# Two rings of three PSUM banks, and one common list of parts, in the slice-weight stage of a graph-network kernel

## The chip, the cores and the metric

The kernel is one program on one core of a Trainium2 chip, launched once. The metric is device time in microseconds (us) from start to end; lower is better. The core has a tensor engine (PE, with its weight loads shown apart as PEld), a vector engine (DVE), a scalar engine (ACT), GpSimd (POOL) and the queue of the sync engine (SP) that issues most of the transfers. Each engine works through its own list of instructions in order and waits for the others on semaphores.

## The reference, cut to what matters

The whole program is two blocks of a graph network on 6250 nodes of 256 features: graph attention, linear attention, a mixture of experts, a relational layer, and at the end a "slice attention". Only the first part of the last one is touched:

```python
# x: [6250, 256], layer-normalised; H = 8 heads, G = D = 64
fx_mid = (x @ W_fx + b_fx)                      # [N, 512]
x_mid  = (x @ W_x + b_x)                        # [N, 512]
slice_weights = softmax((x_mid @ W_slice + b_slice) / temp, axis=-1)
slice_norm  = slice_weights.sum(axis=2)
slice_token = einsum('bhnc,bhng->bhgc', fx_mid, slice_weights)
# then attention among the 64 tokens of each head, and
out_x = einsum('bhgc,bhng->bhnc', out_slice, slice_weights) @ W_out + b_out
```

The kernel has folded W_x, W_slice and the temperature into one matrix of 256x512 beforehand, so a tile of nodes needs one product for its logits, a softmax over groups of 64, and a sum of (features x weights) over all nodes.

## The kernel before

The nodes stand in 50 tiles of 128 rows, two tiles make a pair, and five pairs (slots u = 0 to 4) make a round; there are five rounds. All work of the stage is in `slice_weights`. For each pair and round r there are these parts, and each part runs over the five slots:

- norm: DVE takes the statistics of the loaded rows (L493, L500), ACT the square root (L505), DVE the reciprocal (L509) and the scaled rows xn (L514).
- turn: PE transposes xn into a PSUM bank (L538), ACT copies it to xt (L3542).
- logit0 and logit1, for the first and the second tile of the pair: PE multiplies xt with the logit matrix into a bank (L3594, two matmuls of 128x512); DVE adds the bias out of the bank (L3496), takes the maximum (L3499), subtracts it (L3502); ACT takes the exponential (L3546); DVE sums it (L3505), inverts the sum (L3508) and scales (L3512).
- sum0 and sum1, for the two tiles: PE adds features times weights into the two accumulating banks sum_bank (L3602, two matmuls), and then transposes the weights into a bank (L3610, four transposes); ACT copies that out to slice_t (L3550), which the last stage reads.
- copy: ACT copies xn to xs (L3554), which sum0 and sum1 read.

Of the eight PSUM banks, two are sum_bank, five are `bank[u]`, one for each slot, shared in turn by turn, logit0 and logit1, and one is `turn_bank`, through which all transposes of sum0 and sum1 go one at a time.

The order of the parts on each engine is written out by hand. In the loop, with r the finished round and r+1 the one begun, PE has logit1(r), sum0(r), turn(r+1), logit0(r+1), sum1(r); DVE has norm(r+1), logit1(r), logit0(r+1); ACT has the root of norm(r+1), the copies of sum0(r), turn(r+1), the exponentials of logit1(r), three copies of sum1(r), the exponentials of logit0(r+1), the other two copies of sum1(r), and copy(r+1). The file has two helpers that other stages use and this one does not: `rounds`, which lays out a list of parts on an engine, and `Ring`, which deals a few banks to the slots of several parts in turn.

Of the kernel before, what the change touches and what calls it, by code (L numbers as in the profile page):

```python
# [14 lines left out]
P = 128  # L15
# [3389 lines left out]
def slice_weights(nc, io, dram, keep, logit, tokens, slice_t, sums):  # L3405
# [5 lines left out]
    ALL, HEAD, REST = range(U), range(3), range(3, U)  # L3411
    with ExitStack() as stack:
# [13 lines left out]
        bank = [space.ps(f"bank{u}", [P, 512]) for u in range(U)]  # L3426
        turn_bank = space.ps("turn_bank", [P, 512])
# [6 lines left out]
            space.sems(n, PAIR) for n in ("s_lg", "s_lb", "s_mx", "s_sub", "s_exp", "s_sm", "s_rc", "s_sw", "s_swt", "s_swtc"))  # L3434
        tiles = pair_rows(dram["x3"])
# [16 lines left out]
        with nc.Block() as block:  # L3452
# [17 lines left out]
            def _(dve):  # L3470
# [9 lines left out]
                def part(name, r):  # L3480
# [11 lines left out]
                    elif name in ("logit0", "logit1"):  # L3492
                        i = int(name[-1])
                        for u, n in slots(r):
                            dve.wait_ge(s_lg[i], n)
                            nc.vector.tensor_tensor(sw[:, u, i], bank[u][:, :], b_logit[:, :], ALU.add).then_inc(s_lb[i], 1)  # L3496
# [17 lines left out]

                part("norm", (0, 0))
                part("logit0", (0, 0))
                with dve.Fori(0, ROUNDS - 1) as r:
                    part("norm", (r, 1))
                    part("logit1", (r, 0))
                    part("logit0", (r, 1))  # L3520
                part("logit1", (ROUNDS - 1, 0))
# [8 lines left out]
            def _(act):  # L3530
# [5 lines left out]
                def part(name, r, chosen=ALL):  # L3536
                    for u, n in [slots(r)[k] for k in chosen]:
                        if name == "norm":
                            ln.root(nc, u, n)
                        elif name == "turn":  # L3540
                            act.wait_ge(s_xt, n)
                            nc.scalar.copy(xt[:, u].rearrange("p a n -> p (a n)"), bank[u][:, :]).then_inc(s_xtc, 1)  # L3542
                        elif name in ("logit0", "logit1"):
                            i = int(name[-1])
                            act.wait_ge(s_sub[i], n)
                            nc.scalar.activation(sw[:, u, i], sw[:, u, i], ACT.Exp).then_inc(s_exp[i], 1)  # L3546
                        elif name in ("sum0", "sum1"):
                            i = int(name[-1])
                            act.wait_ge(s_swt[i], n + U)
                            nc.scalar.copy(slice_t[:, tile_at(r, u, i), :].rearrange("p t n -> p (t n)"), turn_bank[:, :]).then_inc(s_swtc[i], 1)  # L3550
                        elif name == "copy":
                            act.wait_ge(s_xn, n + U)
                            act.wait_ge(s_swt[1], n)
                            nc.scalar.copy(xs[:, u, :, 0:D - 1], xn[:, u, :, 0:D - 1]).then_inc(s_copied, 1)  # L3554

                for name in ("norm", "turn", "copy", "logit0"):
                    part(name, (0, 0))
                with act.Fori(0, ROUNDS - 1) as r:
                    part("norm", (r, 1))
                    part("sum0", (r, 0))  # L3560
                    part("turn", (r, 1))
                    part("logit1", (r, 0))
                    part("sum1", (r, 0), HEAD)
                    part("logit0", (r, 1))
                    part("sum1", (r, 0), REST)
                    part("copy", (r, 1))
                part("sum0", (ROUNDS - 1, 0), HEAD)
                part("logit1", (ROUNDS - 1, 0))
                part("sum0", (ROUNDS - 1, 0), REST)
                part("sum1", (ROUNDS - 1, 0))  # L3570

            @block.tensor
            def _(pe):
# [6 lines left out]
                def part(name, r):  # L3580
                    for u, n in slots(r):
                        if name == "turn":
                            pe.wait_ge(s_lb[1], n)
                            pe.wait_ge(s_xn, n + U)
                            transpose_pair(nc, bank[u], xn[:, u], keep["ident"]).then_inc(s_xt, 1)
                        elif name in ("logit0", "logit1"):
                            i = int(name[-1])
                            b = bank[u]
                            if i == 0:
                                pe.wait_ge(s_xtc, n + U)  # L3590
                            else:
                                pe.wait_ge(s_lb[0], n + U)
# [4 lines left out]
                        elif name in ("sum0", "sum1"):  # L3597
# [5 lines left out]
                            if u:  # L3603
                                pe.wait_ge(s_swtc[i], n - 1 + U)
                            elif i == 0:
                                pe.wait_ge(s_swtc[1], n - 1 + U)
                            else:
                                pe.wait_ge(s_swtc[0], n - 1 + U + U)
                            for j in range(J):
                                last = nc.tensor.transpose(turn_bank[:, j * P:(j + 1) * P], sw[:, u, i, j * P:(j + 1) * P], keep["ident"][:, :])  # L3610
                            last.then_inc(s_swt[i], 1)

                part("turn", (0, 0))
                part("logit0", (0, 0))
                with pe.Fori(0, ROUNDS - 1) as r:
                    part("logit1", (r, 0))
                    part("sum0", (r, 0))
                    part("turn", (r, 1))
                    part("logit0", (r, 1))
                    part("sum1", (r, 0))  # L3620
                for name in ("logit1", "sum0", "sum1"):
                    part(name, (ROUNDS - 1, 0))
# [300 lines left out]
```

## Time and profile before

| | us |
|---|---|
| median of 3 runs | 7020.97 (7016.3 to 7034.65) |
| the profiled execution | 7016.3 |
| its span | 7014.5 |
| the loop of the stage and its last round on DVE (6680.36 to 6866.40) | 186.04 |
| mean granted clock of TensorE | 0.864 of full |

Over the whole span PE is busy 75%, DVE 69%, ACT 59% and POOL 52%. These shares average many stages; the stage changed here lies near the end, from about 6642 to 6880 us. After it come only the small work on the tokens and the output. In the rows below the granted clock (PEclk) is 1.00 at 2.4 GHz and 0.50 at 1.2 GHz, the two levels it has.

### The profile page before, as it was taken

The numbers are of one execution on the slowest core, as the hardware profiler recorded it, in microseconds if no ns is written. First come the engines' busy times: TensorE is split into PE (matmuls) and PEld (weight loads), VectorE is DVE, ScalarE is ACT, GpSimd is POOL, SyncE is SP. The second block draws the span as 40 slices with busy tenths as digits, with TensorE's granted clock in tenths as the row PEclk, the third lists the DMA queues.
The fourth block names the chain that finished last, engine by engine and source line by source line (L and its number), as shares of the span: only waits on it lengthen the run. The fifth ranks groups of instructions, "written<-read, shape, count | busy, mean of one in ns | idle before, by whom it ended". The sixth has DMA issues, their size and how long they took to land. (4 is left out here: it accounts for less than half of the span.)

```text
span 7014.5 us, 94498 instructions
## 1 busy us (share of the span) xinstructions
PE 5285.4 (75%) x22314; PEld 3780.4 (54%) x22314; DVE 4842.0 (69%) x13222; ACT 4141.8 (59%) x13411; POOL 3626.7 (52%) x3571
## 2 busy tenths in 40 slices
PE   1768888655888887558888624999998787778698
PEld 1645555434555564535555313888884466555446
DVE  5756666695777777767777687666662487777693
ACT  4568888874899898668998873333335322111142
POOL 3377777727777774477777710000000477777501
PEclk8878888876899998678999866999999898888799
DMA  6444444444444443454444432000006644333402
GB/s 178 120 129 117 118 118 116 111 126 143 117 123 119 123 121 99 129 149 119 125 119 121 112 105 79 28 18 18 18 18 221 206 117 125 109 110 103 128 23 75
DMA packets 483983, 763.48 MB, mean 109 GB/s; under 512 B 85543, under 2 KB 360695, under 8 KB 483511
## 3 DMA queue, kind: packets, MB, share of 16 engines
q0 software_dynamic: 166320, 446.82, 23.3%
q1 hardware_dynamic: 317335, 313.36, 14.2%
q14 instruction: 253, 2.07, 0.1%
q8 instruction: 75, 1.23, 0.1%
HBM read 622.82 MB, written 146.27 MB: 110 GB/s over the span
## 5 line engine op out<-in xcount | busy, mean ns | idle before, releaser
L1806 POOL DMA_INDIRECT gm_got<-scratch_feat,keep_src_tab x2490 | 2485.7, 998 | 776.2 <-issue 668.9
L2028 ACT ACTIVATE gm_got<-gm_got 128x64 f32<-128x64 f32 x9828 | 2393.7, 335 | 5.5 <-DVE gm_got L1941 5.5
L2083 PE MATMUL gm_bank<-gm_got,gm_onehot 128*128 128x264 f32 x4980 | 1777.0, 464 | 401.9 <-DVE gat_acc L1966 236.0
L2083 PEld LDWEIGHTS gm_bank<-gm_got,gm_onehot 128*128 128x128 f32 x4980 | 934.3, 216 | 911.8 <-DVE gat_acc L1966 360.3
L1966 DVE TENSOR_TENSOR gat_acc<-gat_acc,gm_bank 128x264 f32 x2490 | 1060.1, 426 | 506.4 <-PE gm_bank L2083 240.2
L1114 POOL DMA_INDIRECT mix1a_got<-scratch_rel_feat,layer_rel_tab x240 | 238.1, 992 | 1524.8 <-issue 1524.5
L1114 POOL DMA_INDIRECT mix1b_got<-scratch_rel_feat,layer_rel_tab x590 | 583.8, 989 | 189.9 <-issue 186.0
L1171 PE MATMUL mix1b_m_bank<-mix1b_got,mix1b_onehot 128*128 128x256 f32 x1180 | 380.0, 456 | 154.3 <-DVE layer_acc L1145 129.8
L837 POOL DMA_INDIRECT scratch_first<-gat_scores,keep_first_pos x150 | 224.7, 1498 | 461.5 <-DVE gat_scores L820 420.1
L1973 DVE TENSOR_TENSOR gm_onehot<-keep_iota_row,keep_dst_tab 128x896 f32<-128x896 f32 x357 | 386.8, 1084 | 25.8 <-PE gm_bank L2083 22.2
L1171 PEld LDWEIGHTS mix1b_m_bank<-mix1b_got,mix1b_onehot 128*128 128x128 f32 x1180 | 241.0, 222 | 261.1 <-DVE mix1b_onehot L1123 172.7
L3285 ACT ACTIVATE moe_h<-moe_first,moe_shift,moe_gain 128x512 f32<-128x512 f32 (+1 forms) x208 | 147.0, 757 | 346.8 <-PE moe_first L3327 346.8
L3327 PE MATMUL moe_third<-moe_w_high,moe_cuts 128*128 128x256 f32 x1600 | 319.9, 292 | 29.4 <-DVE moe_xh L3213 29.4
L1145 DVE TENSOR_TENSOR layer_acc<-layer_acc,mix1b_m_bank 128x256 f32 x590 | 245.0, 415 | 82.6 <-PE mix1b_m_bank L1171 68.9
L3327 PEld LDWEIGHTS moe_third<-moe_w_high,moe_cuts 128*128 128x128 f32 x1600 | 266.6, 199 | 38.5 <-issue 34.7
L3090 DVE CAST moe_cuts<-moe_h 128x1024 fp32r<-128x1024 f32 (+1 forms) x208 | 140.1, 674 | 194.0 <-ACT moe_h L3285 192.1
L3093 DVE TENSOR_TENSOR moe_cuts<-moe_h,moe_cuts 128x1024 fp32r<-128x1024 f32 (+1 forms) x208 | 246.4, 1184 | 7.1
L3327 PE MATMUL moe_second<-moe_cuts,moe_w_high 128*128 128x512 f32 (+1 forms) x832 | 249.9, 383 | 0.0
L3285 ACT ACTIVATE moe_h<-moe_second,moe_shift,moe_gain 128x512 f32<-128x512 f32 (+1 forms) x208 | 147.0, 758 | 166.6 <-PE moe_second L3327 166.6
L1665 PE MATMUL gm_side<-gm_w,gm_fft 128*128 128x256 f32 x800 | 244.5, 387 | 0.0
L505 ACT ACTIVATE mix1b_ln_std<-mix1b_ln_mv,keep_eps 128x2 f32<-128x2 f32 x75 | 16.8, 286 | 366.3 <-DVE mix1b_ln_mv L500 366.3
L3327 PE MATMUL moe_third<-moe_w_low,moe_cuts 128*128 128x256 f32 x800 | 232.3, 290 | 0.0
(558 smaller groups left out, 10524.4 us busy)
## 6 DMA issues: line engine op xcount, KB each, us to landing
scratch_rel_feat<-rel_out SPq DMA_DIRECT2D x50, 1024.0 KB, 6.3
gm_got<-scratch_feat,keep_src_tab POOLq DMA_INDIRECT x2490, 2.8
gm_flags<-scratch_flags SPq DMA_DIRECT2D x90, 280.0 KB
gf_feat<-scratch_feat SPq DMA_DIRECT2D x75, 256.0 KB, 4.3
gf_old<-scratch_hidden SPq DMA_DIRECT2D x75, 256.0 KB, 4.7
scratch_hidden<-gf_h SPq DMA_DIRECT2D x75, 256.0 KB, 4.4
scratch_feat<-gf_row SPq DMA_DIRECT2D x50, 260.0 KB, 3.8
gm_x<-scratch_x SPq DMA_DIRECT2D x50, 256.0 KB
```

Source lines behind the costliest of these rows:

```text
L1114: nc.gpsimd.indirect_dma_start(out=self.got[:, u, :], out_offset=None, in_=self.table, in_offset=bass.IndirectOffsetOnAxis(ap=self.keep["r ...
L1145: nc.vector.tensor_tensor(rows, rows, self.bank[p % self.BANKS][:, i * D:(i + 1) * D], ALU.add).then_inc(self.s_acc, 1)
L1171: last = self.nc.tensor.matmul(self.bank[p % self.BANKS][:, i * D:(i + 1) * D], self.onehot[:, u, :], self.got[:, u, :], start=True, stop= ...
L1665: nc.tensor.matmul(out, self.fft[:, c, i * P:(i + 1) * P], self.w2[:, c, :], start=(c == 0), stop=False)
L1806: nc.gpsimd.indirect_dma_start(out=got[:, place // GROUPS, place % GROUPS * GROUP + j, 0:GAT_ROW], out_offset=None, in_=dram["feat"][layer ...
L1966: nc.vector.tensor_tensor(a, a, bank[j % BANKS][:, 0:GAT_SUM], ALU.add).then_inc(s_acc, 1)
L1973: nc.vector.tensor_tensor(onehot[:, half:half + GROUP, :], keep["iota_row"][:, :].unsqueeze(1).to_broadcast([P, GROUP, P]), keep["dst_tab" ...
L2028: last = nc.scalar.activation(rows, rows, ACT.Copy, scale=got[:, b, i, D + h:D + h + 1])
L2083: nc.tensor.matmul(bank[i % BANKS][:, 0:GAT_SUM], onehot[:, i % HOTS, :], got[:, v[1] % B, i, :], start=True, stop=True).then_inc(s_sum, 1)
L3093: return nc.vector.tensor_tensor(out, whole, high.bitcast(F32), ALU.subtract)
L3285: last = nc.scalar.activation((h1, h2)[j][:, e % 2, a, 0:size * P], (bank1, bank2)[j][a][:, 0:size * P], ACT.Relu, bias=shift[:, j, q:q + ...
L3327: last = nc.tensor.matmul(out, lhs(k)[i], rhs(k)[j], start=(p == 0), stop=(p == len(passes) - 1))
```

## The change

PE, DVE and ACT now take the same lists of parts through `rounds` (FIRST before the loop, BODY in it, LAST behind it), each engine doing what is its own in each part. The banks become two rings of three: `early` for turn and logit0, `late` for logit1, sum0 and sum1. A slot takes the next bank of its ring, and PE waits until the last user of that bank has been read out.

```diff
-    ALL, HEAD, REST = range(U), range(3), range(3, U)
+    FIRST, LAST = ["norm", "turn", "logit0", "copy"], ["logit1", "sum0", "sum1"]
+    BODY = [("logit1", 0), ("norm", 1), ("sum0", 0), ("turn", 1), ("logit0", 1), ("sum1", 0), ("copy", 1)]
...
-        bank = [space.ps(f"bank{u}", [P, 512]) for u in range(U)]
-        turn_bank = space.ps("turn_bank", [P, 512])
+        bank = [space.ps(f"bank{u}", [P, 512]) for u in range(6)]
...
+        early = Ring(bank[0:3], {"turn": s_xtc, "logit0": s_lb[0]})
+        late = Ring(bank[3:6], {"logit1": s_lb[1], "sum0": s_swtc[0], "sum1": s_swtc[1]})
+        ring = {n: q for q in (early, late) for n in q.names}
...
 (DVE)
-                part("norm", (0, 0))
-                part("logit0", (0, 0))
-                with dve.Fori(0, ROUNDS - 1) as r:
-                    part("norm", (r, 1))
-                    part("logit1", (r, 0))
-                    part("logit0", (r, 1))
-                part("logit1", (ROUNDS - 1, 0))
+                rounds(dve, part, FIRST, BODY, LAST)
...
 (ACT)
-                for name in ("norm", "turn", "copy", "logit0"):
-                    part(name, (0, 0))
-                with act.Fori(0, ROUNDS - 1) as r:
-                    part("norm", (r, 1))
-                    part("sum0", (r, 0))
-                    part("turn", (r, 1))
-                    part("logit1", (r, 0))
-                    part("sum1", (r, 0), HEAD)
-                    part("logit0", (r, 1))
-                    part("sum1", (r, 0), REST)
-                    part("copy", (r, 1))
...
+                rounds(act, part, FIRST, BODY, LAST)
...
 (PE, turn)
-                            pe.wait_ge(s_lb[1], n)
                             pe.wait_ge(s_xn, n + U)
-                            transpose_pair(nc, bank[u], xn[:, u], keep["ident"]).then_inc(s_xt, 1)
+                            transpose_pair(nc, early.enter(pe, name, u, n), xn[:, u], keep["ident"]).then_inc(s_xt, 1)
 (PE, logit0 and logit1)
-                            b = bank[u]
-                            if i == 0:
-                                pe.wait_ge(s_xtc, n + U)
-                            else:
-                                pe.wait_ge(s_lb[0], n + U)
+                            b = ring[name].enter(pe, name, u, n)
+                            pe.wait_ge(s_xtc, n + U)
 (PE, sum0 and sum1, between the two sums and the four transposes)
-                            if u:
-                                pe.wait_ge(s_swtc[i], n - 1 + U)
-                            elif i == 0:
-                                pe.wait_ge(s_swtc[1], n - 1 + U)
-                            else:
-                                pe.wait_ge(s_swtc[0], n - 1 + U + U)
+                            b = late.enter(pe, name, u, n)
```

The existing helpers that it now calls:

```python
def rounds(engine, part, first, body, last):
    for name in first:
        part(name, (0, 0))
    with engine.Fori(0, ROUNDS - 1) as r:
        for name, ahead in body:
            part(name, (r, ahead))
    for name in last:
        part(name, (ROUNDS - 1, 0))

class Ring:                      # place(): the bank and its last user
    s, size = self.names.index(name) * UNROLL + u, len(self.banks)
    before, rounds_back = [q for q in range(s) if q % size == s % size], 0
    ...
    q = before[-1]
    return self.banks[s % size], self.left[q // UNROLL], (rounds_back - shift) * UNROLL + u - q % UNROLL
                                 # enter(): wait until that user's bank was read out
    bank, left, behind = self.place(name, u)
    pe.wait_ge(left, n + (UNROLL - behind))
```

The number of instructions is the same. On ACT, in the loop, the order before is this (L505 root, L3550 copy of the transposed weights, L3542 copy of xt, L3546 exponential of logit1 first and of logit0 second; a row without a count is the first of its group, whose other rows are left out):

```order
L505 ACT_TABLE_LOAD
L505 ACTIVATE slw_ln_std<-slw_ln_mv,keep_eps 128x2
...
L3550 COPY ffn_slice_t<-slw_turn_bank 128x512
...
L3542 COPY slw_xt<-slw_bank 128x512 x5
...
L3546 ACT_TABLE_LOAD
L3546 ACTIVATE slw_sw<-slw_sw 128x512
...
L3550 COPY ffn_slice_t<-slw_turn_bank 128x512
...
L3546 ACTIVATE slw_sw<-slw_sw 128x512 x5
```

In the changed program the same engine has, in the loop (L3543 is now the exponential, L3547 the copy of the transposed weights, L3539 the copy of xt):

```order
L3543 ACTIVATE slw_sw<-slw_sw 128x512
...
L505 ACT_TABLE_LOAD
L505 ACTIVATE slw_ln_std<-slw_ln_mv,keep_eps 128x2
...
L3547 COPY ffn_slice_t<-slw_bank 128x512
...
L3539 COPY slw_xt<-slw_bank 128x512 x5
L3543 ACT_TABLE_LOAD
L3543 ACTIVATE slw_sw<-slw_sw 128x512 x5
...
L3547 COPY ffn_slice_t<-slw_bank 128x512
```

The exponentials of logit1(r) moved from behind the copies of sum0(r) to the very front of the loop, ahead of the root of norm(r+1), and all copies of sum1(r) now stand behind the exponentials of logit0(r+1). DVE's list turned in the same way: logit1(r) before norm(r+1) instead of behind it.

On PE the sequence of parts is the same, but the banks are others. Before, logit1 and the first transposes of sum0, in the loop:

```order
L3594 MATMUL slw_bank0<-logit_w,slw_xt 128x512 x2
...
L3594 MATMUL slw_bank3<-logit_w,slw_xt 128x512 x2
...
L3594 MATMUL slw_bank4<-logit_w,slw_xt 128x512 x2
...
L3602 MATMUL slw_sum_bank0<-slw_sw,slw_xs 128x512
...
L3610 MATMUL slw_turn_bank<-keep_ident,slw_sw 128x128 x4
```

In the changed program (L3573 is logit1, L3584 the transposes of sum0, slots 0 to 4 in order):

```order
L3573 MATMUL slw_bank3<-logit_w,slw_xt 128x512 x2
...
L3573 MATMUL slw_bank5<-logit_w,slw_xt 128x512 x2
...
L3573 MATMUL slw_bank3<-logit_w,slw_xt 128x512 x2
...
L3573 MATMUL slw_bank4<-logit_w,slw_xt 128x512 x2
...
L3584 MATMUL slw_bank5<-keep_ident,slw_sw 128x128 x4
...
L3584 MATMUL slw_bank3<-keep_ident,slw_sw 128x128 x4
...
L3584 MATMUL slw_bank4<-keep_ident,slw_sw 128x128 x4
...
L3584 MATMUL slw_bank5<-keep_ident,slw_sw 128x128 x4
```

Slot 3 of logit1 takes the bank of its slot 0, and slot 3 of sum0 the bank of its slot 0.

## Rows read from the trace of the kernel before

**Rows 1.** Busy time by stretch: us, then PE, PEld, DVE, ACT, POOL (instructions), PEclk, DMA
```profile
6721.65:6763.96 42.31, 41.40 (x142) 21.30 (x141) 39.16 (x97) 20.13 (x37) 0.00 (x0) 1.00 0.10 31
6680.36:6866.40 186.04, 178.01 (x601) 91.33 (x600) 172.53 (x412) 84.59 (x158) 0.00 (x0) 0.99 0.07 21
```

**Rows 2.** Timeline of DVE, one loop turn: start us, us, instruction, [idle before <-releaser]
```profile
6721.65 3.36 DVE L493 BATCH_NORM_STATS2 slw_ln_stats<-slw_x 128x6 f32<-128x256 f32 x10
...
6729.59 3.08 DVE L3496 TENSOR_TENSOR slw_sw<-slw_bank,logit_b 128x512 f32<-128x512 f32 x5
...
6741.72 3.06 DVE L3505 TENSOR_REDUCE slw_den<-slw_sw 128x8 f32<-128x512 f32 x5 [3.09 <-ACT slw_sw L3546]
...
6748.37 3.08 DVE L3496 TENSOR_TENSOR slw_sw<-slw_bank,logit_b 128x512 f32<-128x512 f32 x5
...
6754.32 3.10 DVE L3502 TENSOR_TENSOR slw_sw<-slw_sw,slw_top 128x512 f32<-128x512 f32 x5
...
6763.96 3.36 DVE L493 BATCH_NORM_STATS2 slw_ln_stats<-slw_x 128x6 f32<-128x256 f32 x10
```

**Rows 3.** Timeline of ACT, the same turn
```profile
6725.19 1.04 ACT L505 ACTIVATE slw_ln_std<-slw_ln_mv,keep_eps 128x2 f32<-128x2 f32 x5 [3.64 <-DVE slw_ln_mv L500]
...
6737.19 2.55 ACT L3542 COPY slw_xt<-slw_bank 128x512 f32<-128x512 f32 x5
6739.77 1.28 ACT L3546 ACT_TABLE_LOAD   x1
...
6755.04 3.04 ACT L3546 ACTIVATE slw_sw<-slw_sw 128x512 f32<-128x512 f32 x5 [0.51 <-DVE slw_sw L3502]
6757.99 0.57 ACT L3550 COPY ffn_slice_t<-slw_turn_bank 128x512 f32 x1
```

**Rows 4.** Timeline of PE, the same turn
```profile
6734.26 1.88 PE L3602 MATMUL slw_sum_bank<-slw_sw,slw_xs 128*128 128x512 f32 x4
6735.98 0.60 PE L3610 MATMUL slw_turn_bank<-keep_ident,slw_sw 128*128 128x128 f32 x4
6736.42 2.35 PE L538 MATMUL slw_bank<-keep_ident,slw_xn 128*128 128x128 f32 x20
6738.60 8.75 PE L3594 MATMUL slw_bank<-logit_w,slw_xt 128*128 128x512 f32 x20
6747.19 1.88 PE L3602 MATMUL slw_sum_bank<-slw_sw,slw_xs 128*128 128x512 f32 x4
```

**Rows 5.** Timeline of all engines, the last logit1: its matmuls and adds
```profile
6843.38 8.75 PE L3594 MATMUL slw_bank<-logit_w,slw_xt 128*128 128x512 f32 x20
...
6852.16 0.69 DVE L3496 TENSOR_TENSOR slw_sw<-slw_bank,logit_b 128x512 f32<-128x512 f32 x1 [1.02 <-PE slw_bank L3594]
```

**Rows 6.** Timeline of PE, from the start of the stage to the first stall
```profile
6653.28 4.50 PE L538 MATMUL slw_bank<-keep_ident,slw_xn 128*128 128x128 f32 x20 [6.52 <-DVE slw_xn L514]
6657.57 18.14 PE L3594 MATMUL slw_bank<-logit_w,slw_xt 128*128 128x512 f32 x40
...
6685.45 0.66 PE L3610 MATMUL slw_turn_bank<-keep_ident,slw_sw 128*128 128x128 f32 x4 [3.47 <-ACT ffn_slice_t L3550]
```

**Rows 7.** Busy time by stretch, around the two restarts of PE (columns as in rows 1)
```profile
6652.00:6658.00 6.00, 4.72 (x21) 4.66 (x22) 3.69 (x13) 2.81 (x7) 0.00 (x0) 0.50 0.74 204
6658.00:6660.00 2.00, 2.00 (x4) 0.72 (x3) 0.00 (x0) 2.00 (x5) 0.00 (x0) 0.70 0.67 223
...
6686.00:6690.00 4.00, 4.00 (x11) 2.09 (x10) 4.00 (x11) 0.58 (x1) 0.00 (x0) 0.57 0.67 216
6690.00:6880.00 190.00, 182.89 (x622) 93.78 (x621) 166.27 (x381) 85.36 (x155) 0.00 (x0) 1.00 0.05 16
```

**Rows 8.** Timeline of DVE: the first add, and the first norm of the loop
```profile
6660.30 0.69 DVE L3496 TENSOR_TENSOR slw_sw<-slw_bank,logit_b 128x512 f32<-128x512 f32 x1 [4.57 <-PE slw_bank L3594]
...
6680.36 3.35 DVE L493 BATCH_NORM_STATS2 slw_ln_stats<-slw_x 128x6 f32<-128x256 f32 x10
```

**Rows 9.** Timeline of DVE, the end of the stage
```profile
6876.69 1.29 DVE L3527 COPY ffn_sums<-slw_sum_bank 128x512 f32<-128x512 f32 x2 [9.07 <-PE slw_sum_bank L3624]
```

More of the change, by code:

```diff
@@ L3495, in part @@
                             dve.wait_ge(s_lg[i], n)
-                            nc.vector.tensor_tensor(sw[:, u, i], bank[u][:, :], b_logit[:, :], ALU.add).then_inc(s_lb[i], 1)
+                            nc.vector.tensor_tensor(sw[:, u, i], ring[name].bank(name, u)[:, :], b_logit[:, :], ALU.add).then_inc(s_lb[i], 1)
                         for u, n in slots(r):
@@ L3534, in _, with part @@
                     act.sem_inc(s_swtc[i], U)
-                def part(name, r, chosen=ALL):
-                    for u, n in [slots(r)[k] for k in chosen]:
+                def part(name, r):
+                    for u, n in slots(r):
                         if name == "norm":
@@ L3541, in part @@
                             act.wait_ge(s_xt, n)
-                            nc.scalar.copy(xt[:, u].rearrange("p a n -> p (a n)"), bank[u][:, :]).then_inc(s_xtc, 1)
+                            nc.scalar.copy(xt[:, u].rearrange("p a n -> p (a n)"), early.bank(name, u)[:, :]).then_inc(s_xtc, 1)
                         elif name in ("logit0", "logit1"):
@@ L3602, in part @@
                                 nc.tensor.matmul(sum_bank[a][:, :], xs[:, u, i, a * P:(a + 1) * P], sw[:, u, i], start=False, stop=False)
-                            if u:
-                                pe.wait_ge(s_swtc[i], n - 1 + U)
-                            elif i == 0:
-                                pe.wait_ge(s_swtc[1], n - 1 + U)
-                            else:
-                                pe.wait_ge(s_swtc[0], n - 1 + U + U)
+                            b = late.enter(pe, name, u, n)
                             for j in range(J):
-                                last = nc.tensor.transpose(turn_bank[:, j * P:(j + 1) * P], sw[:, u, i, j * P:(j + 1) * P], keep["ident"][:, :])
+                                last = nc.tensor.transpose(b[:, j * P:(j + 1) * P], sw[:, u, i, j * P:(j + 1) * P], keep["ident"][:, :])
                             last.then_inc(s_swt[i], 1)
[L3613 to L3622, printed above, removed]
+                rounds(pe, part, FIRST, BODY, LAST)
                 for a in range(HALVES):
```

6 lines of the change are left out of this document (1 added, 5 removed).

## The prediction

> **What bounds the kernel now.** First the page: no engine bounds the whole span, so a change in one stage is read from that stage. Next the busy time by stretch. In one loop turn of 42.31 us PE is busy 41.40 us and DVE 39.16 us [rows 1]. Both are nearly full: PE has almost no slack to absorb a new wait, and DVE only 3 us. Then the timeline of DVE over that turn: norm takes 6729.59 - 6721.65 = 7.94 us; the second logit part, which meets no wait, takes 6763.96 - 6748.37 = 15.59 us; the first one has 3.09 us of idle time in it, waiting for the exponentials [rows 2], because ACT stands in the copies of turn and in a table load first [rows 3]. So 7.94 + 2 x 15.59 + 3.09 = 42.2 us is a turn (42.31 in the row), and DVE, with this one wait, sets it. From the first norm of the loop [rows 8] to the end of the last logit1 there are 186.04 us [rows 1].
>
> Prices used below, all at full clock. A slot of logits on PE: (6747.19 - 6738.60) / 5 = 1.72 us. A slot of sums is 6735.98 - 6734.26 = 1.72, its transposes 0.44, together 2.16 [rows 4]. From the first matmul of logit1 (6843.38) to the add of its slot 4 (6852.16) is 8.78 us, less four slots of 1.72 is 1.9 for the first slot's product until its add can start [rows 5]; with the weight load ahead of it I take 2.1 from release to add. Adds follow each other by 0.60 (3.08 for five) when nothing waits [rows 2]. From the last add's start to the end of its part: 15.59 - 4 x 0.60 = 13.2 us.
>
> **The change part by part.** The instructions are the same in number and form, so only waits change. I write N for the start of a norm on DVE, and follow one turn.
>
> *1. The exponentials of logit1 come first on ACT.* The wait of 3.09 us [rows 2] goes. Gain 3.1 us a turn.
>
> *2. The copies of sum0(r) now come behind a root that comes late.* Before, norm stood ahead of logit1 on DVE, and the root ended at 6726.23, when sum0 began on PE; now norm(r+1) stands behind logit1(r), while sum0(r) on PE follows directly on the products of logit1(r). The root ends 6726.23 - 6721.65 = 4.6 us after N [rows 2, 3]. PE can do slots 0 to 2 of sum0 into the three late banks and the two sums of slot 3; then it waits for the bank of slot 0, which ACT empties at N + 4.6 + 0.6 = N + 5.2 [rows 3]. Behind this wait on PE stand: transposes of slot 3 (to 5.7), sums of slot 4 (to 7.4), its transposes (to 7.9), turn(r+1), then logit0(r+1). ACT copies slot 4 at 8.2 to 8.8, and xt of slots 0, 1, 2 until 10.4 (2.55 us for five [rows 3]). The first logit0 needs bank 2, which held turn's slot 2, so it starts at N + 10.45 and DVE can add at N + 12.55. But norm ends at N + 7.94. DVE idles 4.6 us, where before it had logit1 to do. Cost 4.6 us a turn.
>
> *3. logit0 is now paced by PE.* DVE arrives before the products, so its five adds come every 1.72 us, not every 0.60: 4 x 1.12 = 4.5 us a turn. Slots 3 and 4 also need the banks of slots 0 and 1, added out by then, so the ring itself adds nothing here. The first adds of the kernel before show this pace already, the first at 6660.30 [rows 8]. The last add starts at N + 19.4, and logit0's part ends at N + 32.6.
>
> *4. sum1(r) waits for the exponentials of logit0(r+1).* PE ends logit0 at N + 19.05, does three slots of sum1 and two sums (to 27.2), and waits until ACT, whose exponentials start 0.7 us after the subtraction (6755.04 against 6754.32) and take 3.04 [rows 2, 3], has copied slot 0, at N + 27.4: almost no wait. sum1 ends at N + 30.05, and logit1(r+1) begins. Its first add could come at 32.15; DVE is there at 32.6. Slot 1 could be added at 33.9, slot 2 at 35.6, slot 3 at 37.35, slot 4 at 39.05, all paced by PE again. Had PE been early, slot 3 would have waited for DVE, for the bank of slot 0. The five adds take 6.45 us to the start of the last instead of 2.4: cost 4.05 us. The next norm starts at N + 39.05 + 13.2 = N + 52.25.
>
> The sum of a turn: 42.2 - 3.1 + 4.6 + 4.5 + 4.05 = 52.25 us, against 42.2. PE, after logit1 at 38.65, has filled the ring at 46.8 and stalls until 52.25 + 5.2 = 57.45, so 10.6 us in each turn.
>
> *5. The clock after the stall.* Before, PE restarted after 6.52 us of idle at 6653.28 [rows 6]; the granted clock was 0.50 until 6658 and 0.70 on average in the next 2 us, so about 5.6 us at half. After the 3.47 us stall that ended at 6685.45 [rows 6], it was 0.57 over 6686 to 6690, some 3.4 us at half; with no such stall later it stayed 1.00 [rows 7]. Stalls of 10.6 us lie beyond both. Half clock for 3.4 to 5.6 us holds back 1.7 to 2.8 us of work, and what follows the restart is the chain of step 2 up to DVE's first add. I take 2.5 us a turn; the lowest is nothing (full clock), the highest 5.2, if half clock lasts until 1.8 us into logit0, as it did at the start (matmuls from 6657.57, full clock by about 6659.2).
>
> *6. The first turn.* DVE now does logit1(0) at 6680.36 instead of norm. PE finished slots 0 to 2 of it near 6672.2, since logit0 and logit1 ran from 6657.57 to 6675.7 [rows 6] without stopping, and slot 3 waits for DVE's add, 6680.36 + 0.7. Released at 6681.1, slot 3 is added at 6683.2 and slot 4 at 6684.9, and the part ends at 6698.1: 17.75 us instead of 15.6. PE has idled 9 us by then, so I add the 2.5 us of step 5 here too. The xs copy, now behind the exponentials, is done some 6 us before sum0 needs it: nothing.
>
> *7. The end.* The last round has no norm, so ACT reaches sum0's copies when its exponentials are done, 5.9 us before the end of logit1. Sums and transposes of sum1 and the closing matmuls remain behind DVE's last scaling as before, when ffn_sums was read at 6876.69 [rows 9], 10.3 us after 6866.40. Nothing, with bounds of 1 us either way.
>
> The sum, from 6680.36: 17.75 for logit1(0), and 4 turns of 52.25 = 209.0, the last of which ends with logit1(4). That is 226.75 against 186.04: +40.7 at full clock. Five restarts by 2.5 add 12.5: +53.2. On the profiled execution's 7016.3 (2 us more than its span of 7014.5) this gives 7069.5; its median of three is 7020.97, 4.7 above, so I forecast 7073, from a base of 7020 just under the median.
>
> The ring should have been a gain at one place: transposes through one bank met an ACT wait of 0.9 to 3.5 us [rows 6], and in the first turn that stall vanishes; it is within the sum already, since the sum does not inherit it.
>
> **The rivals.**
> *A. Full clock after the stalls.* If PE comes back at full clock, only the waits remain: 7020 + 41 = 7061. Against it: both restarts in the rows were followed by half clock.
>
> *B. Half clock until logit0.* The late transposes and turn follow on each other behind the stall, and at the start of the stage half clock held through all of turn [rows 6, 7]. If only the plain matmuls of logits bring the clock back, turn's slots cost 0.88 instead of 0.44, logit0 starts at N + 14.7 instead of 10.45, and its first add comes 5.2 us late. 4 x 5.2 + 2.5 = 23.3 over +40.7: 7020 + 64 = 7084. Against it: two long sums of slot 4 come ahead of turn. The Trainium skill, in "TensorE: Matmul & The Clock Gate", Part 4: PE-mode transpose, says that a transpose does not count as PE-busy in the way a matmul does; it speaks for this rival, and the trace at the start of the stage, 0.50 during 4.3 us of nothing but transposes, agrees.
>
> *C. Not slower: the stalls of the ring stay away.* If ACT's copies of sum0 did not wait for DVE (the root early enough) then steps 2 to 4 would fall, PE would never stand, and a turn would be PE's 41.4 us [rows 1] or less: 4 x 0.8 us, and 3.5 us of the first stall, faster, 7014. It decides if PE reaches slot 3 of sum0 later than N + 5.2; by my count it is there 5.4 us before N. Little speaks for it.
>
> *D. No change: half of the chain is hidden.* If DVE did not idle after norm and one of the two add parts ran at 0.60, the turn would lose 4.05 or 4.5 less 3.1, so 1 to 2 us: 7020 + 6 = 7027. It needs PE ahead of DVE, and PE stalls.
>
> **How the numbers follow.** A measurement here tells about 0.3%, 21 us, from no change. The forecast has 0.60, A 0.14, B 0.16, C 0.04, D 0.06. Slower is the first three, 0.90. C and D as worked out both lie within 0.3%, but C could be larger than its count, for which I take 0.02 of it: same 0.08, faster 0.02. The range runs from A with the lower base and a few us off, 7052, to B with the upper, 7092; C and D are left out.
>
> **What would show it.** In the profile after, DVE's loop turn should be 52 to 57 us. PE should have one idle of 10 to 11 us a turn, on the transposes of sum0 released by ACT's copy; ACT should wait for DVE's statistics there. DVE should idle 4 to 10 us before the first add of logit0, then show adds 1.7 us apart in both logit parts, and no wait for the exponentials in logit1. The granted clock should drop to 0.5 after each stall and be near 1 for the rest. If the turn is about 42 us, the ring was not full, and steps 2 to 4 are wrong; if it is 52 with a clock of 1.00, only step 5 is.

## The result, and the profile after

The changed kernel is slower. Its median is 7072.59 us (7068.94 to 7077.59, four runs), and that of the kernel before, run beside it, 7018.64 (7013.7 to 7034.65, four runs). The ratio is 1.0078, with a 95% interval from 1.0065 to 1.0091, so the loss is 54 us, between 46 and 64. Eleven more executions of the changed kernel are on record, from 7072.27 to 7087.27; the median of all fifteen is 7076.93. Forecast were 7073, between 7052 and 7092.

| | before, us | after, us | difference | forecast |
|---|---|---|---|---|
| median | 7018.64 | 7072.59 | +54.0 | +53 |
| the profiled execution | 7016.3 | 7087.3 | +71.0 | |
| first matmul of sum_bank to the copy into ffn_sums | 6642.98 to 6876.69 = 233.71 | 6664.73 to 6947.78 = 283.05 | +49.3 | +53.2 |
| the loop with its last round, on DVE | 186.04 | 236.92 | +50.9 | +53.2 |

The profiled executions differ by more than the medians. Some 21.75 us of it lie before the stage, in code that both kernels share (DVE reaches the stage at 6642.73 and at 6664.48), and say nothing of the change. The part of the stage ahead of the loop, in which DVE also waits for the first rows to be loaded, took 37.38 us before and 35.84 after, in the same order of parts; so the whole stage grows by 1.6 us less than the loop. Everything below is read inside the stage.

Busy time by stretch of the changed kernel (us, then PE, PEld, DVE, ACT, POOL, granted clock, DMA): the whole loop, one turn, and three stretches behind PE's stall in that turn. They answer to [rows 1, 7].

```profile
6700.57:6937.49 236.92, 195.33 (x617) 100.24 (x618) 175.39 (x411) 85.28 (x159) 0.00 (x0) 0.89 0.05 17
6720.87:6774.65 53.78, 43.57 (x140) 22.19 (x140) 39.90 (x97) 19.88 (x37) 0.00 (x0) 0.91 0.08 25
6726.00:6730.00 4.00, 4.00 (x8) 2.11 (x9) 2.88 (x9) 1.46 (x3) 0.00 (x0) 0.50 0.48 146
6730.00:6732.00 2.00, 2.00 (x17) 1.71 (x15) 0.00 (x0) 0.93 (x2) 0.00 (x0) 0.90 0.91 293
6732.00:6742.00 10.00, 9.96 (x32) 4.89 (x31) 2.77 (x4) 3.39 (x6) 0.00 (x0) 1.00 0.04 15
```

DVE is busy 39.90 us of the turn, where it was 39.16, so its work is the same; the turn grew from 42.31 to 53.78 around it. Neither engine is full any more: PE is busy 43.57 of 53.78.

The timeline of DVE shows where the 11.5 us went. First the part in front of the loop's first norm, then one turn; it answers to [rows 2, 8].

```profile
6700.57 1.87 DVE L3499 TENSOR_TENSOR slw_sw<-slw_bank,logit_b 128x512 f32<-128x512 f32 x3
6705.19 0.69 DVE L3499 TENSOR_TENSOR slw_sw<-slw_bank,logit_b 128x512 f32<-128x512 f32 x1 [2.75 <-PE slw_bank L3573]
6707.64 0.69 DVE L3499 TENSOR_TENSOR slw_sw<-slw_bank,logit_b 128x512 f32<-128x512 f32 x1 [1.76 <-PE slw_bank L3573]
...
6720.87 3.35 DVE L493 BATCH_NORM_STATS2 slw_ln_stats<-slw_x 128x6 f32<-128x256 f32 x10
...
6725.56 3.32 DVE L514 TENSOR_SCALAR slw_xn<-slw_x,slw_ln_mv,slw_ln_rstd 128x256 f32<-128x256 f32 x10
6735.20 0.69 DVE L3499 TENSOR_TENSOR slw_sw<-slw_bank,logit_b 128x512 f32<-128x512 f32 x1 [6.32 <-PE slw_bank L3573]
6736.92 0.69 DVE L3499 TENSOR_TENSOR slw_sw<-slw_bank,logit_b 128x512 f32<-128x512 f32 x1 [1.02 <-PE slw_bank L3573]
...
6742.07 0.69 DVE L3499 TENSOR_TENSOR slw_sw<-slw_bank,logit_b 128x512 f32<-128x512 f32 x1 [1.02 <-PE slw_bank L3573]
...
6748.65 3.05 DVE L3508 TENSOR_REDUCE slw_den<-slw_sw 128x8 f32<-128x512 f32 x5
...
6755.27 0.68 DVE L3499 TENSOR_TENSOR slw_sw<-slw_bank,logit_b 128x512 f32<-128x512 f32 x1
6756.28 0.69 DVE L3499 TENSOR_TENSOR slw_sw<-slw_bank,logit_b 128x512 f32<-128x512 f32 x1 [0.33 <-PE slw_bank L3573]
...
6761.43 0.69 DVE L3499 TENSOR_TENSOR slw_sw<-slw_bank,logit_b 128x512 f32<-128x512 f32 x1 [1.02 <-PE slw_bank L3573]
...
6774.65 3.35 DVE L493 BATCH_NORM_STATS2 slw_ln_stats<-slw_x 128x6 f32<-128x256 f32 x10
```

Four things stand in it. The sum of the exponentials (L3508) has no wait: the 3.09 us of before are gone. Between the norm and the first add DVE is idle 6.32 us. The five adds of logit0 take 6742.07 - 6735.20 = 6.87 us from first start to last, not 2.40, so +4.47; the five of logit1 take 6.16, so +3.76. And -3.09 + 6.32 + 4.47 + 3.76 = 11.46 us, which is the growth of the turn (53.78 - 42.31 = 11.47). The other three turns take 54.19, 54.25 and 54.40, with 6.72 to 6.96 of idle before logit0.

The timelines of PE and ACT in the same turn name what DVE waits for; they answer to [rows 4] and [rows 3].

```profile
6701.38 6.22 PE L3573 MATMUL slw_bank<-logit_w,slw_xt 128*128 128x512 f32 x8 [8.89 <-DVE slw_sw L3499]
...
6713.90 1.88 PE L3581 MATMUL slw_sum_bank<-slw_sw,slw_xs 128*128 128x512 f32 x4
6725.96 1.11 PE L3584 MATMUL slw_bank<-keep_ident,slw_sw 128*128 128x128 f32 x4 [10.18 <-ACT ffn_slice_t L3547]
6726.87 3.62 PE L3581 MATMUL slw_sum_bank<-slw_sw,slw_xs 128*128 128x512 f32 x4
6730.28 0.66 PE L3584 MATMUL slw_bank<-keep_ident,slw_sw 128*128 128x128 f32 x4
6730.78 2.63 PE L538 MATMUL slw_bank<-keep_ident,slw_xn 128*128 128x128 f32 x20
6733.24 8.79 PE L3573 MATMUL slw_bank<-logit_w,slw_xt 128*128 128x512 f32 x20
```

```profile
6711.93 3.04 ACT L3543 ACTIVATE slw_sw<-slw_sw 128x512 f32<-128x512 f32 x5 [14.65 <-DVE slw_sw L3505]
6714.98 1.28 ACT L505 ACT_TABLE_LOAD   x1
6724.40 1.04 ACT L505 ACTIVATE slw_ln_std<-slw_ln_mv,keep_eps 128x2 f32<-128x2 f32 x5 [8.14 <-DVE slw_ln_mv L500]
6725.35 1.53 ACT L3547 COPY ffn_slice_t<-slw_bank 128x512 f32 x3
```

Slots 0, 1 and 2 of sum0 had long been transposed, but ACT stood 8.14 us before the root, waiting for DVE's statistics, and copied them only at 6725.35. PE waited 10.18 us for the first of those copies, did the two sums of the last slot in 3.62 us in place of 1.88, and reached logit0 at 6733.24. The waits, added up over the stage (us in total, times, longest), say the same.

```profile
DVE slw_sw L3499 <- PE slw_bank L3573: 69.7, 43, 7.0
...
PE slw_bank L3584 <- ACT ffn_slice_t L3547: 40.7, 4, 10.2
```

### The profile page after: what moved, and what is told of

The parts are those of the page before. It is cut to its first block and busy times, and to the rows that moved or that the text cites. A ratio compares the mean times of both kernels' runs of the same rounds, so it can differ in the third digit from the quotient of the medians.

```text
span 7085.5 us, 94548 instructions
## 1 busy us (share of the span) xinstructions
PE 5313.8 (75%) x22314; PEld 3799.3 (54%) x22314; DVE 4842.8 (68%) x13222; ACT 4142.8 (58%) x13411; POOL 3639.1 (51%) x3571
## 5 line engine op out<-in xcount | busy, mean ns | idle before, releaser
L3767 POOL TENSOR_TENSOR slo_x<-slo_x,slo_b_out 128x512 f32<-128x512 f32 x25 | 31.0, 1269 | 419.3 <-DMA slo_x<-scratch_x 419.3
L505 ACT ACTIVATE mix1b_ln_std<-mix1b_ln_mv,keep_eps 128x2 f32<-128x2 f32 x75 | 16.8, 286 | 381.2 <-DVE mix1b_ln_mv L500 381.2
```

## The experiments

Each kernel differs from the changed one by the edit shown. The stage is the time from the first matmul of sum_bank to the copy into ffn_sums, 233.7 us in the kernel before and 283.0 after. The first six ran on chips on which the whole program takes 7911 to 7922 us: there the gathers ahead of the stage wait longer (1214 us idle on their line in e1, 776 in the kernel before as first profiled). The slots in the stage take the same 1.72 us, so the stage and the ratio are compared, not the times. The ratios rest on 4 to 12 executions each and are good to 8 to 20 us. Stage and turns are read from one profiled execution of each kernel, and 35.0 to 37.5 us of every stage lie ahead of the loop, where no experiment moves work; a difference of 2 us between two stages says nothing.

| label | median, us | before beside it | ratio (95%) | stage, us | turns, us |
|---|---|---|---|---|---|
| e1_lists_only | 8001.68 | 7911.15 | 1.0120 (1.0103 to 1.0137) | 322.6 | 62.7 to 64.3 |
| e2_rings_only | 7970.16 | 7911.15 | 1.0082 (1.0058 to 1.0105) | 297.3 | 58.0 to 58.2 |
| e3_norm_first | 7935.15 | 7911.15 | 1.0041 (1.0025 to 1.0058) | 263.6 | 49.0 to 50.2 |
| e4_sum0_first | 7947.75 | 7911.15 | 1.0054 (1.0036 to 1.0073) | 269.0 | 50.7 to 51.1 |
| e5_filler | 7969.10 | 7922.19 | 1.0072 (1.0047 to 1.0097) | 281.2 | 51.6 |
| e6_late4 | 7950.74 | 7922.19 | 1.0041 (1.0027 to 1.0056) | 272.6 | 51.5 to 52.2 |
| e7_one_ring | 7042.91 | 7036.47 | 1.0009 (0.9998 to 1.0020) | 238.7 | 43.2, the first 45.0 |
| e8_one_ring_lists | 7069.73 | 7036.47 | 1.0052 (1.0035 to 1.0070) | 271.1 | 51.8 to 53.2 |

### The two halves of the change, each by itself

e1_lists_only keeps the new lists and goes back to the banks of before, with their waits on PE:

```diff
-        bank = [space.ps(f"bank{u}", [P, 512]) for u in range(6)]
+        bank = [space.ps(f"bank{u}", [P, 512]) for u in range(U)]
+        turn_bank = space.ps("turn_bank", [P, 512])
```

> The changed kernel's lists of parts (logit1 ahead of norm, the sum0 copies on ACT behind the root) with the banks of the kernel before (five for turn and logits, one for all transposed weights). Theory 'order' (the lists cause the loss, the rings soften it): behind the stall on ACT's copy four slots of sum0 remain instead of one, the first add of logit0 comes about 3.9 us later than in the changed kernel, sum1 meets a second stall of about 4 us until the exponentials of logit0 are done, and a loop turn is 61 to 63 us instead of 54.2; the first logit1 is 15.6 us, not 20.3. In all 4 x 62 + 15.6 - 186 = +78, about 7097 us. Theory 'rings' (three banks a ring cause the loss): without the rings the turn goes back to 42 to 44 us, 7020 to 7028 us. A half-and-half story would give something near 7045.

e2_rings_only keeps the two rings of three and goes back to the orders of before on DVE, ACT and PE:

```diff
-                rounds(dve, part, FIRST, BODY, LAST)
+                with dve.Fori(0, ROUNDS - 1) as r:
+                    part("norm", (r, 1))
+                    part("logit1", (r, 0))
+                    part("logit0", (r, 1))
...
-                rounds(act, part, FIRST, BODY, LAST)
+                (the order of the kernel before)
```

> The changed kernel's two rings of three banks with the hand-written lists of the kernel before on PE, DVE and ACT. Theory 'order': were the lists the whole cause, the turn would be 42 us and the time 7019 us. Theory 'rings': PE can do only three slots of logit1 ahead, then stands behind DVE's norm until the first add of logit1, about 9.5 us idle in a turn, and the chain PE sum0, turn, copies of xt, exponentials of logit1 follows it; worked through like the prediction this gives a turn of 50.4 us at full clock and about 53 with half clock after the stall, 7052 to 7062 us. If both theories hold, each edit is bad by itself and the two losses don't add up, since in the changed kernel DVE reaches logit1 right away.

Measured: the lists alone lose 88.9 us in the stage, the rings alone 63.6, and both together 49.3. Neither half is harmless, and they don't add up: the rings hold off part of what the lists do. In e1 the idle time moved as the theory says. With one bank for all transposes PE stands after the first slot of sum0, not the third, so more of sum0 is left behind the late root. PE's timeline in e1:

```profile
7619.00 1.88 PE L3583 MATMUL slw_sum_bank<-slw_sw,slw_xs 128*128 128x512 f32 x4
7635.36 1.11 PE L3591 MATMUL slw_turn_bank<-keep_ident,slw_sw 128*128 128x128 f32 x4 [14.48 <-ACT ffn_slice_t L3545]
...
7663.92 0.66 PE L3591 MATMUL slw_turn_bank<-keep_ident,slw_sw 128*128 128x128 f32 x4 [4.01 <-ACT ffn_slice_t L3545]
```

The second row is a second stall, in sum1, behind the exponentials of logit0: the rings of three hide that one in the changed kernel. DVE idles 10.92 us before logit0 and 5.13 before logit1. The loss came out above the 78 us expected: the turns are 62.7 to 64.3 us long and not 62, and DVE waits 16.08 us for the last sums, not 9.07, because the second stall also stands in the last round.

In e2 the turn came out at 58 us, where about 53 was expected. That expectation had one ring wait and the trace has two. PE's timeline, then DVE's, in one turn of e2:

```profile
7627.46 5.28 PE L3594 MATMUL slw_bank<-logit_w,slw_xt 128*128 128x512 f32 x8 [7.20 <-DVE slw_sw L3500]
...
7656.05 6.35 PE L3594 MATMUL slw_bank<-logit_w,slw_xt 128*128 128x512 f32 x8 [4.87 <-DVE slw_sw L3500]
```

```profile
7631.07 0.69 DVE L3500 TENSOR_TENSOR slw_sw<-slw_bank,logit_b 128x512 f32<-128x512 f32 x1 [2.54 <-PE slw_bank L3594]
...
7648.66 3.06 DVE L3509 TENSOR_REDUCE slw_den<-slw_sw 128x8 f32<-128x512 f32 x5 [9.22 <-ACT slw_sw L3550]
...
7659.86 0.69 DVE L3500 TENSOR_TENSOR slw_sw<-slw_bank,logit_b 128x512 f32<-128x512 f32 x1 [2.68 <-PE slw_bank L3594]
```

Slot 3 of logit1 waits for DVE's add out of slot 0's bank, behind a norm (7.20 us). So sum0 and turn come late, ACT's copies of them too, and with them the exponentials behind them: DVE waits 9.22 us, where it was 3.09 [rows 2]. Then slot 3 of logit0 waits in the other ring in the same way, 4.87 us, which I had not counted.

### Where the new lists lose

The theory puts the loss on the place of norm: the root on ACT, and xn behind it, are late for a PE that has nothing else. e3 and e4 move one part each in the list.

```diff
-    BODY = [("logit1", 0), ("norm", 1), ("sum0", 0), ("turn", 1), ("logit0", 1), ("sum1", 0), ("copy", 1)]
+    BODY = [("norm", 1), ("logit1", 0), ("sum0", 0), ("turn", 1), ("logit0", 1), ("sum1", 0), ("copy", 1)]
```

> The changed kernel with norm at the head of the common list: DVE has norm, logit1, logit0 as before the change, ACT has root, exponentials of logit1, copies of sum0, turn. Theory: DVE has logit1 to do while PE prepares logit0, so its idle time before the first add of logit0 falls from about 6.7 to about 2 to 4 us, while PE waits for DVE's first adds of logit1 (stall about 6 us) and ACT's sum0 copies hardly hold it. A turn of 47.7 us at full clock, about 50 with half clock: 7045 to 7055 us. Rival, the place of norm does not matter and only the pace of PE against the rings does: 54 us a turn, 7073 us.

```diff
-    BODY = [("logit1", 0), ("norm", 1), ("sum0", 0), ("turn", 1), ("logit0", 1), ("sum1", 0), ("copy", 1)]
+    BODY = [("logit1", 0), ("sum0", 0), ("norm", 1), ("turn", 1), ("logit0", 1), ("sum1", 0), ("copy", 1)]
```

> The changed kernel with one move in the list: sum0 ahead of norm, so that ACT copies sum0 out before it takes the root. On PE and DVE nothing moves. Theory (step 2 of the prediction: sum0's rest stands behind the root): PE finishes sum0 before norm ends, and waits for xn instead; behind the restart only turn and logit0 remain, the first add of logit0 comes about 2.2 us earlier, the turn is about 51.9 instead of 54.2, 4 x 2.3 = 9 us less than the changed kernel: about 7064 us. Rival, the idle of DVE behind norm comes only from logit0 following norm directly and the copies don't matter: 7073 us. Rival the other way, the copies are the whole of it: 4 x 6.7 = 27 less, 7046 us.

Both went the way of the theory, and both gained somewhat more than was counted. e4 only lets ACT copy sum0 before the root; its turn is 51.0 and not 54.2, where 51.9 was expected, and its stage is 14 us shorter and not 9. That is neither nothing nor the 27 us of the two rivals. e3's turn of 49.0 to 50.2 is the 50 expected. PE no longer waits there, but next for xn itself, by its timeline:

```profile
7576.84 4.02 PE L538 MATMUL slw_bank<-keep_ident,slw_xn 128*128 128x128 f32 x20 [7.98 <-DVE slw_xn L514]
```

With the copies out of the way the stall is 7.98 us in place of 10.18, and DVE still idles 3.25 us before logit0. Only in e3, where logit1 stands between norm and logit0, does that idle shrink to about 1.7 (2 to 4 were expected). Its turn (50.17 us from 7594.53) stays 7.9 us above 42.31, and DVE's rows give 7.3 of it: the ring holds slots 3 and 4 of logit1 (2.75 and 1.84 us), logit0 waits 1.70, its other adds four times 1.03, and the 3.09 us for the exponentials are gone.

```profile
7607.10 0.69 DVE L3499 TENSOR_TENSOR slw_sw<-slw_bank,logit_b 128x512 f32<-128x512 f32 x1 [2.75 <-PE slw_bank L3573]
7609.63 0.69 DVE L3499 TENSOR_TENSOR slw_sw<-slw_bank,logit_b 128x512 f32<-128x512 f32 x1 [1.84 <-PE slw_bank L3573]
7624.63 0.69 DVE L3499 TENSOR_TENSOR slw_sw<-slw_bank,logit_b 128x512 f32<-128x512 f32 x1 [1.70 <-PE slw_bank L3573]
7626.35 0.69 DVE L3499 TENSOR_TENSOR slw_sw<-slw_bank,logit_b 128x512 f32<-128x512 f32 x1 [1.03 <-PE slw_bank L3573]
```

### What the clock adds

e5_filler leaves the waits and fills the stall: eleven matmuls of 128x512 that add zeros to the accumulating banks, between the sums of slot 3 and the wait for its bank.

```diff
+                            if i == 0 and u == 3:
+                                for k in range(11):
+                                    nc.tensor.matmul(sum_bank[k % HALVES][:, :], nothing[:, :], w_logit[:, 0, :], start=False, stop=False)
                             b = late.enter(pe, name, u, n)
```

> The changed kernel with 11 matmuls of 128x512 by a weight tile of zeros into the accumulating banks (they add nothing) in each sum0 part, between the sums of slot 3 and its wait for the bank: 11 x 0.86 = 9.5 us of work inside the stall of 10.2 us. Theory (step 5: half clock after the stall costs 2 to 2.5 us a turn): the granted clock stays 1.00 through the loop, the first add of logit0 comes 12.5 us after the start of norm instead of 14.3 to 15.0, the turn is 52.2 instead of 54.2, 7 to 8 us less than the changed kernel: about 7065 us. The last round has no such stall, so there the filler costs up to 5 us of PE time ahead of sum1, if PE has no slack: then 7070 us. Rival, the clock does not matter to the turn: 7073 to 7078 us, turn 54.2.

One turn of e5 by busy time, and in PE's timeline the restart:

```profile
7600.49:7652.11 51.62, 50.84 (x164) 25.37 (x163) 39.90 (x96) 19.78 (x37) 0.00 (x0) 1.00 0.08 26
```

```profile
7605.59 0.66 PE L3587 MATMUL slw_bank<-keep_ident,slw_sw 128*128 128x128 f32 x4 [0.74 <-ACT ffn_slice_t L3547]
7606.08 1.88 PE L3581 MATMUL slw_sum_bank<-slw_sw,slw_xs 128*128 128x512 f32 x4
...
7610.71 8.78 PE L3573 MATMUL slw_bank<-logit_w,slw_xt 128*128 128x512 f32 x20
```

The granted clock is 1.00, the sums behind the stall take 1.88 us again, and all four turns are 51.60 to 51.62. The mean of the changed kernel's four is 54.15, so the clock is worth 54.15 - 51.62 = 2.5 us a turn. The median gains little by it, because the same matmuls stand in the last round too, where they lengthen the end: DVE waits 18.30 us for the last sums, not 9.07 [rows 9]. That is 9.2 us, almost all of the filler, where up to 5 were expected. It takes back nearly what the four turns gain, so the times do not show the price of the clock; the turns do.

### What the ring adds

e6_late4 takes a bank from `early` and gives it to `late`:

```diff
-        early = Ring(bank[0:3], {"turn": s_xtc, "logit0": s_lb[0]})
-        late = Ring(bank[3:6], {"logit1": s_lb[1], "sum0": s_swtc[0], "sum1": s_swtc[1]})
+        early = Ring(bank[0:2], {"turn": s_xtc, "logit0": s_lb[0]})
+        late = Ring(bank[2:6], {"logit1": s_lb[1], "sum0": s_swtc[0], "sum1": s_swtc[1]})
```

> The changed kernel with the six banks dealt two to the early ring (turn, logit0) and four to the late one (logit1, sum0, sum1). Theory (the order makes the stall, the size of a ring only moves it by a slot): sum0 gets its slot 3 and the sums of slot 4 done ahead of the stall, turn with two banks goes at the pace of ACT's copies; the first add of logit0 comes 0.4 us earlier at full clock, up to 2 us earlier where half clock held the sums back; the first logit1 of the loop meets the stall only at slot 4, 1.7 us sooner done. Turn 52.5 to 54, about 7065 us, between 7060 and 7072. Rival, the size of the late ring is the bound: a bank more would take a fourth slot of 2.2 us out of the stall in each of the parts, 4 x 4.3 = 17 us, 7055 us.

e7 and e8 deal the six banks in one ring over all five parts, in the order in which PE comes to them; e7 with the orders of before, e8 with the new lists. The first and the last round lack some of the parts, so both also make PE wait once ahead of the loop, for all adds of the first logit0, and in the last round for all copies of sum0 ahead of sum1's transposes.

```diff
-        early = Ring(bank[0:3], {"turn": s_xtc, "logit0": s_lb[0]})
-        late = Ring(bank[3:6], {"logit1": s_lb[1], "sum0": s_swtc[0], "sum1": s_swtc[1]})
+        early = late = Ring(bank, {"logit1": s_lb[1], "sum0": s_swtc[0], "turn": s_xtc, "logit0": s_lb[0], "sum1": s_swtc[1]},
+                            ahead=["turn", "logit0"])
```

> The hand-written lists of the kernel before, with one ring of six banks dealt over all five parts in the order in which PE comes to them (logit1, sum0, turn, logit0, sum1), instead of five banks by slot and one for the transposes. A slot then waits for the user six places back on PE, which by the kernel before's own rows is always read out in time, except logit1's slot 0, which gets the bank that sum1's slot 4 just left (about 1 us). Theory (a ring harms only where it is dealt so that a slot waits for an engine that is late; three banks split off for logit1 were the harm in the rings-only run): turn 42 to 43 us, the stall of 3.5 us in the first turn gone, stage (first matmul to ffn_sums) 230 to 237 us against 233.7 before and 297 with the two rings of three; time within 0.1% of the kernel before. Rival: rings on these banks cost by themselves (more register work on PE, banks shared by engines): turn over 46 us, stage over 250.

> The changed kernel's common lists, with the one ring of six banks in PE's order. Theory (the lists alone, without a bank wait in the way, leave DVE with nothing between norm and logit0): sum0 is done ahead of the stall, PE then waits for xn, turn and logit0 follow; first logit1 15.6 us (no ring wait), first add of logit0 10 us after the start of norm at full clock and about 12 at half, turn 50.5 to 52.5, stage 264 to 273 us against 283 for the changed kernel: so the lists alone cost some 30 to 38 us over the kernel before, about 0.45%. Rival: the loss of the changed kernel is in the dealing of the banks: stage under 245 us.

With the new lists, the stage shrinks as the banks behind sum0 grow: 322.6 with one (e1), 283.0 with three, 272.6 with four (e6). e6 gained more than was expected: its turns are 51.5 to 52.2 us and not 52.5 to 54, and its ratio, 1.0041 (at most 1.0056), is below the 1.0057 that 7060 us would be. The first logit1 of its loop takes 17.9 us and not 20.3. The loop is 12 us shorter than that of the changed kernel, between the 8 of the theory and the 17 of the rival, so the size of the ring matters more than the theory allowed. But six banks in one ring give 271.1, no more than four: there PE waits for xn, not for a bank (7.97 us), as in e4.

So of the 49.3 us that the change costs, 37.4 stay (271.1 - 233.7) with the banks in one ring, and 12 go. These 12 do not belong to the rings alone: e4 keeps the rings of three and gets to 269.0 by ACT's order, so they are the price of a ring of three together with copies that stand behind a late root. Of the rest, the place of norm holds a good part: e3, with the rings of three, is only 29.9 us above the kernel before.

With the orders of before the same six banks in one ring cost nothing that the ratio can tell (e7). Its stage, 238.7, is a little over the 230 to 237 expected, and its loop takes 192.8 us in the trace against 186.0. More than half of these 6.8 us is in the first turn, 45.0 us against 41.3: the stall of 3.47 us that was to go gave way to one of 7.05, in which slot 1 of sum0 waits for the bank that DVE reads only behind its norm, and DVE then waits 5.79 us for the exponentials, not 2.06.

```profile
6694.29 1.12 PE L3609 MATMUL slw_bank<-keep_ident,slw_sw 128*128 128x128 f32 x4 [7.05 <-DVE slw_sw L3500]
```

In its steady turns the wait for the exponentials is 3.96 us, where it was 3.09, because PE waits 1.04 us for a copy by ACT ahead of logit1 and 0.75 for an add ahead of a transpose:

```profile
6751.57 3.06 DVE L3509 TENSOR_REDUCE slw_den<-slw_sw 128x8 f32<-128x512 f32 x5 [3.96 <-ACT slw_sw L3550]
```

```profile
6769.02 8.85 PE L3594 MATMUL slw_bank<-logit_w,slw_xt 128*128 128x512 f32 x20 [1.04 <-ACT ffn_slice_t L3554]
6782.48 0.66 PE L3609 MATMUL slw_bank<-keep_ident,slw_sw 128*128 128x128 f32 x4 [0.74 <-DVE slw_sw L3500]
```

No version beat the kernel before. Its turn of 42.31 us holds 41.40 of PE work [rows 1], so less than a microsecond a turn was there to win.

## Why the prediction was right

*Step 1, the exponentials first: -3.1 a turn.* Right. The wait is gone in all turns.

*Step 2, the copies of sum0 behind a late root: +4.6 at full clock.* Right in mechanism and nearly in size. The root came 6724.40 - 6720.87 = 3.5 us after the norm and ended at 4.6, as counted; PE stood 10.18 us where 10.6 was forecast. Without the clock's part DVE idled 4.15 us in e5. e4 shows that the copies are only part of the cause: with them out of the way xn is next, and 3.25 us of idle stay. The prediction named the copies alone; by it, moving them would have taken away the whole wait.

*Step 3, logit0 paced by PE: +4.5.* Measured +4.47.

*Step 4, logit1 paced by PE: +4.05.* Measured +3.76. The wait for the exponentials in sum1 was nothing, as said. DVE had its first product waiting and the second 0.33 us late, so one of four gaps was shorter.

*Step 5, the clock: +2.5, between 0 and 5.2.* Measured 2.5 by e5, as the mean of four turns. The size was a choice within wide bounds, so that it came out so exactly is partly luck. By its own rows the first restart was at half clock for 5.9 us, not 5.6 (4.7 until 6658, and 1.2 of the next 2 us at a mean of 0.70). The idle before logit0 in the changed kernel agrees: 6.32 to 6.96, less the 4.15 of e5, is 2.2 to 2.8.

*Step 6, the first turn: 17.75 at full clock, 20.25 with the clock's part.* Measured 20.30 (6700.57 to 6720.87), the mean clock in it 0.84.

*Step 7, the end: nothing.* 6947.78 - 6937.49 = 10.3 us, as before.

The loop was forecast at +53.2 and measured at +50.9. The 2.3 us between them are four turns of 54.15 where 54.75 was said (steps 2 and 4). The medians differ by 54.0; the 3 to 5 us above what the stage shows are inside the interval of the ratio. That the forecast of 7073 lies within 1 us of the median of 7072.59 is luck: the loop was forecast 2.3 us too long, the base 1.4 us too high, and the median of all fifteen executions is 4 us higher.

*The rivals.* A, full clock after the stalls, would have given turns of 52.25 and 1.00 in the row of the stretch; the row has 0.50 over 6726 to 6730. That A's waits alone cost nearly what was worked out, e5 confirms, with turns of 51.6. B, half clock until logit0, falls by the same rows: 0.90 over 6730 to 6732, where PE did the tail of the sums and then transposes, and turn's twenty transposes took 2.63 us, as they take in e5 at full clock, not 4.50 as at the start of the stage [rows 6]. But the sums came ahead of turn here, so this alone does not say whether transposes bring the clock back. In e4 turn's transposes follow the stall by themselves, and the clock came back while PE did nothing else. Busy time by stretch of e4, the transposes that start at 7576.84, and the logits behind them:

```profile
7578.50:7580.00 1.50, 1.50 (x9) 1.50 (x8) 0.87 (x3) 0.96 (x3) 0.00 (x0) 0.50 0.88 300
7580.00:7580.70 0.70, 0.70 (x8) 0.70 (x7) 0.00 (x0) 0.53 (x2) 0.00 (x0) 0.86 0.89 304
7580.70:7583.00 2.30, 2.30 (x8) 1.10 (x7) 0.39 (x1) 2.12 (x3) 0.00 (x0) 1.00 0.78 256
```

So the clock rose behind nothing but transposes. It does not always do so within twenty of them: in the first turn of e8, after a stall of 12.58 us, they took 4.50 us at a granted clock of 0.51, as at the start of the stage. The Trainium skill, in "TensorE: Matmul & The Clock Gate", Part 4: PE-mode transpose, says that a transpose does not count as PE-busy in the way a matmul does, and I had read that as speaking for B; the rows of e4 speak against it, and the measurement decides. Rivals C and D needed a PE that doesn't stand, and it stands in every turn.

What stays open: DVE's list and ACT's list were never put back apart, so the shares of the two in the 37.4 us are not known. Nor is it shown how much of e3's remaining 29.9 us would go with one ring. The medians of the changed kernel and of the one before also hold what lies ahead of the stage, which no run here explains.

## What to carry to other kernels

When one list of parts is given to several engines, look at what each engine has left to do while a chain crosses between them: here DVE's norm, ACT's root, xn, turn, the copy and logit0 form such a chain, and logit1 between norm and logit0 was what covered it. When banks are dealt in rings, count for every part the slot at which the ring is full, and which engine empties it behind what; a ring of three under parts of five slots tied PE to the reader twice in each turn of e2 (7.20 and 4.87 us), while one ring over all parts in PE's order held it for 1.04 and 0.75 us in a steady turn of e7. A stall of PE on the chain costs its length and then the clock: add a term for it, and bound it by the restarts that the trace before already shows. To measure that term, fill the stall with work that changes nothing and read the turn, and leave the filler out of a round that has no stall.

## What the runs showed of the hardware

After a stall of 10.18 us the granted clock was 0.50, the 1.2 GHz level, over 6726 to 6730 and 0.90 over the next 2 us; the two sums of a slot took 3.62 us in place of 1.88. The price at the end of the chain was 2.2 to 2.8 us a turn (turns of 53.78 to 54.40 us against 51.6 in e5). Stalls of 7.51 and 8.02 us (e6) show the same slower transposes at the restart, 1.12 us for four in place of 0.60.

The fall can also come after the restart. In e1, after a stall of 4.01 us, the clock was 1.00 over the first 0.49 us (7663.92 to 7664.41) and 0.59 over the next 2.9; in the kernel before, after 3.47 us, it was 1.00 over 6685.45 to 6686 and 0.57 over the next 4 us.

How long the lower level lasts is not fixed. In e1, after stalls of 14.48 and 14.49 us, the sums at the restart took 3.62 us one turn and 2.83 the next, and the turns of that kernel scatter between 62.7 and 64.3 by it, while those of e5, without low clock, agree within 0.02 us.
